# First strip of a two-layer graph kernel: rows gathered at once into idle tiles, low parts partly on GpSimd, setup in few wide operations

## The chip, the cores and the metric

The kernel runs on one core of a Trainium2 chip. The metric is the device time of one execution in microseconds, lower is better; the number compared is the median of several runs.

The engines are TensorE (PE, with its weight loads PEld), VectorE (DVE), ScalarE (ACT), GpSimd (POOL) and SyncE (SP, which here only issues transfers). Each works through its own instructions in order; semaphores tie them together.

## The reference, cut to what matters

Two graph attention layers over 10,000 nodes and 20,000 edges (10,000 drawn ones, sorted by destination, and one self loop per node), then a small feed-forward block:

```python
xn = layernorm(x)                                  # x: [10000, 768] f32
def gat(x, W, a_src, a_dst, b, heads, d_out, concat):
    h = (x @ W).reshape(N, heads, d_out)
    e = leaky_relu(einsum(h, a_src)[src] + einsum(h, a_dst)[dst], 0.2)
    alpha = softmax_over_edges_of_each_dst(e)      # segment max, exp, segment sum
    out = segment_sum(alpha[:, :, None] * h[src], dst)
    return (out.reshape(N, heads * d_out) if concat else out.mean(axis=1)) + b
h = elu(gat(xn, W1, ..., heads=4, d_out=512, concat=True))   # [10000, 2048]
x = x + gat(h, W2, ..., heads=1, d_out=768, concat=False)
out = x + ffn(layernorm(x))                        # 768 -> 96 -> 768, gelu
```

The kernel moves the weighted sum ahead of the first product: for each head it computes z = sum over edges of alpha * xn[src], and then z @ W1. Numbers are kept to near f32 precision by writing each f32 operand as a high and a low f16 part and adding three f16 products (high*high, high*low, low*high).

## The kernel before, in words

Stages follow each other with a barrier between: logits of layer 1, softmax over edges (it leaves one record of 16 numbers per edge in DRAM), `stage_layers` (both matrix products, by far the longest), a second softmax, and the output stage. The change is inside `stage_layers`, and there only in its beginning.

`stage_layers` works in 20 strips of 500 nodes (`NS`, `SN`). A strip has 10 windows of 50 nodes (`WPS`, `WN`). One window's tile has 128 partitions: 78 for edges that end in the window and 50 for its own nodes. For each window q, i:

- `load_slots` (L1142) brings the ten records tiles into `slots`, one transfer each, and the nodes' mean and 1/deviation by one transfer from `logit1` (L1148). In the first strip ACT issues half of the records (L1462).
- `slot_math` (L1242) makes the ten columns of row indices `idx`, and `mean`, `scale`, `bias`. Then come ten masks (L1273), ten look-up products on PE (L1480), the weights and their halves `wh`, `wl` (L1278 to L1282).
- `gather` on POOL (L1195) fetches 128 rows of x by index into `raw[:, i % 2]`, a tile with two buffers. A buffer is free again when the window two before has been multiplied (`z_done`).
- `high_rows` on ACT (L1433) writes the normalised rows as f16 into `rows_hi[:, i % 2]`; `low_rows` on DVE (L1267, L1268) normalises `raw` in place and subtracts the high part, in place again (`rows_lo` is the same memory as `raw`).
- `spread` on DVE (L1289 to L1293) makes the 128 x 200 weight tiles `ah`, `al`.
- `window` on PE (L1491) makes 18 products of 128x128 by 128x200 into the three banks `pz`; ACT takes each bank's high part to `zh` (L1425) and DVE its low part to `zl` (L1298).

In strips 1 to 19 the windows are made beside the products of the strip before. The ten windows of the first strip (L1399 to L1411, L1464 to L1468, L1562) have no such cover: nothing else runs, and the first product of `body(0)` (L1524) starts behind them. The order of DVE in that loop, by window i, is: rows of i+1, low parts of i, spread of i+2. ACT's is: high rows of i+1, high parts of i.

The tiles `gh` and `gl` (128 x 16 x 504 f16 each) are the input of the second layer's product. They are first written in `body(0)`, and stand idle while the first strip's windows are made. Their four last columns are only zeroed (L1219, L1221).

Ahead of all this DVE sets up constants (L1217 to L1239), 93 instructions, most of them one column wide; the semaphore `init` reaches 3 behind the last of them, and SP and ACT wait for it before they load records, since the records land in the tile `slots`, which these instructions write.

Of the kernel before, what the change touches and what calls it, by code (L numbers as in the profile page):

```python
# [24 lines left out]
ALU = mybir.AluOpType  # L25
ACT = mybir.ActivationFunctionType
# [995 lines left out]

STEPS = NT * KC
XPER = 25
AT_STEP = {1 + 6 * i: i for i in range(WPS)}
# [67 lines left out]
def stage_layers(nc, c, io, dr):  # L1093
    with ExitStack() as ctx:
# [12 lines left out]
        step_off, step_self = m.sb("step_off", [128, 1]), m.sb("step_self", [128, 1])  # L1107
        place, posi = m.sb("place", [128, 1]), m.sb("posi", [128, 128], I32)
        pos = m.sb("pos", [128, 128])
        idx = m.sb("idx", [128, WPS], I32)  # L1110
# [23 lines left out]
            "h2_out", "scale_ready", "hi_done", "normed", "lo_done", "xrows_ready"))  # L1134
        b2_in, x_copied = m.sem("b2_in"), m.sem("x_copied")
        block = ctx.enter_context(nc.Block())
# [5 lines left out]
        def _(sp):  # L1142
            def load_slots(q, first):
                if not first:
                    sp.wait_ge(a_ready, WPS * q)
                for i in range(WPS // 2 if first else WPS):
                    load_records(sp, c, LAYER1, dr.rec1, slots, slots_in, WPS * q + i, i)
                sp.dma_start(slots[WE:128, :, 11:13],  # L1148
                             dr.logit1[bass.ds(SN * q, SN), 2 * HEADS:TW1].rearrange("(i p) w -> p i w", p=WN),
                             allow_slow_non_contiguous=True).then_inc(slots_in, 16)  # L1150

# [20 lines left out]
            sp.dma_start(b2[:, 0:D], io["b2"].rearrange("(a d) -> a d", a=1).broadcast_to([128, D])).then_inc(b2_in, 16)  # L1172
            sp.wait_ge(init, 3)
            load_slots(0, True)
# [8 lines left out]
        @block.gpsimd  # L1183
        def _(pool):
            nc.gpsimd.iota(posi[:], pattern=[[1, 128]], base=-WE, channel_multiplier=0).then_inc(posed, 1)
            nc.gpsimd.iota(idx[:, 0:1], pattern=[[0, 1]], base=-WE, channel_multiplier=1).then_inc(posed, 1)

            def hold(sem, value):

                pool.wait_ge(sem, value)  # L1190
                pool.sem_inc(held, 1)

            pool.wait_ge(posed, 2)

            def gather(q, first):  # L1195
                hold(idx_ready, q + 1)
                for i in range(WPS):
                    if not (first and i < 2):
                        hold(z_done, 3 * (WPS * q + i - 1))
                    nc.gpsimd.indirect_dma_start(raw[:, i % 2, :], None, io["x"][:, :], bass.IndirectOffsetOnAxis(  # L1200
                        ap=idx[:, i:i + 1], axis=0), bounds_check=N - 1, oob_is_err=False).then_inc(gathered[i % 2], 16)

            def extra_chunk(i, w, k):
                hold(xidx_ready, 2 * k + 2)
                nc.gpsimd.indirect_dma_start(raw[:, 0, :], None, io["x"][:, :], bass.IndirectOffsetOnAxis(
                    ap=xidx[:, 0:1], axis=0), bounds_check=N - 1, oob_is_err=False).then_inc(xgathered, 16)

            gather(0, True)
            windows_with_extras(pool, c, LAYER1, 0, WPS, extra_chunk)
            with pool.Fori(1, NS) as q:  # L1210
                gather(q, False)
                windows_with_extras(pool, c, LAYER1, WPS * q, WPS, extra_chunk)

        @block.vector
        def _(dve):

            ch = Chain(dve, setup)  # L1217
            nc.vector.memset(raw[:], 0.0).then_inc(init, 1)
            nc.vector.memset(gh[:, :, SN:], 0.0).then_inc(init, 1)  # L1219
            nc.vector.memset(b2[:, D:W2C], 0.0)  # L1220
            nc.vector.memset(gl[:, :, SN:], 0.0)  # L1221
            dve.wait_ge(posed, 2)
            ch.put(nc.vector.tensor_copy(pos[:], posi[:]))
            ch.put(nc.vector.memset(slots[:], 0.0))
            ch.link(nc.vector.tensor_copy(place[:], idx[:, 0:1]))
            ch.put(nc.vector.tensor_scalar(is_self[:], place[:], 0.0, None, ALU.is_ge))
            ch.link(nc.vector.tensor_scalar(is_edge[:], place[:], 0.0, None, ALU.is_lt))
            ch.put(nc.vector.tensor_scalar(step_off[:], is_edge[:], float(-SN), None, ALU.mult))
            ch.put(nc.vector.tensor_scalar(step_self[:], is_self[:], float(SN), None, ALU.mult))
            nc.vector.memset(xslots[:], 0.0).then_inc(xslots_free, 1)  # L1230
# [8 lines left out]
            nc.vector.memset(near[:], 0.0).then_inc(init, 1)  # L1239
            per = 13 + WPS  # L1240

            def slot_math(qc, q, first):  # L1242

                dve.wait_ge(slots_in, 16 * (WPS + 1) * (q + 1))
                if not first:
                    for b in range(2):
                        dve.wait_ge(gathered[b], 16 * (WPS // 2) * q)
                qc.put(nc.vector.tensor_tensor(rel[:], slots[:, :, 9], woff[:], ALU.add))
# [102 lines left out]
            def body(s, first, last):  # L1351
                q = s + 1
                gc = Chain(dve, chain, KC * s)
                qc = Chain(dve, setup, q * per + ch.n)
                rc = Chain(dve, normed, WPS * q)
                for k in range(KC):
# [46 lines left out]
            spread(qc, 0, 1, True)  # L1403
            rc = Chain(dve, normed)
            low_rows(rc, 0, 0)
            for i in range(WPS):
                if i + 1 < WPS:
                    low_rows(rc, 0, i + 1)
# [12 lines left out]
        def _(act):  # L1421
# [6 lines left out]
            def high_rows(q, i):  # L1428

                if i < 2:  # L1430
                    act.wait_ge(scale_ready, q + 1)
                act.wait_ge(gathered[i % 2], 16 * (WPS // 2) * q + 16 * (i // 2 + 1))
                nc.scalar.activation(rows_hi[:, i % 2], raw[:, i % 2], ACT.Identity, bias=bias[:, i:i + 1],  # L1433
# [26 lines left out]

            act.wait_ge(init, 3)
            for i in range(WPS // 2, WPS):  # L1462
                load_records(act, c, LAYER1, dr.rec1, slots, slots_in, i, i)
            high_rows(0, 0)  # L1464
            for i in range(WPS):
                if i + 1 < WPS:
                    high_rows(0, i + 1)
                high_parts(0, i)  # L1468
# [6 lines left out]
        def _(pe):  # L1475
# [5 lines left out]

            def window_products(d, b):

                o = pz[d // 2][:, d % 2 * HEADS * WN:(d % 2 + 1) * HEADS * WN]
                high, low = (part[:, b, 128 * d:128 * d + 128] for part in (rows_hi, rows_lo))
                flat = lambda t: t[:, b].rearrange("p h n -> p (h n)")
# [4 lines left out]
            def window(q, i, first):  # L1491
# [4 lines left out]
                for k in range(3):  # L1496
                    if not (first and i == 0):
                        pe.wait_ge(zl_ready, 3 * (WPS * q + i - 1) + k + 1)
                    for d in (2 * k, 2 * k + 1):
                        ins = window_products(d, i % 2)  # L1500
                    ins.then_inc(z_done, 1)
# [60 lines left out]
            for i in range(WPS):  # L1562
                window(0, i, True)
            pe.wait_ge(zl_ready, 3 * WPS)
            z_extras(0, None)
            body(0, True, False)
# [569 lines left out]
```

## Time and profile before

| | |
|---|---|
| median of 3 runs | 4033.67 us (4027.44 to 4034.61) |
| the profiled execution | 4030.57 us, of which its span 4028.8 us |
| stage_layers: first instruction | 447.66 us |
| last setup instruction of DVE ends | 455.44 us |
| first gather issued on POOL | 466.35 us |
| first window product on PE | 475.79 us |
| last low part of the ten windows ends | 529.14 us |
| first product of the first strip's body | 530.99 us |

The times in the last six lines are read from the timeline, as microseconds from the span's start. The timeline has one line per group of instructions: start, duration, engine, line of the kernel, operation, output and inputs, shapes, count, and in brackets how long the engine sat idle before it and what released it. Over the whole span PE is busy 89%, DVE 61%, ACT 38% and POOL 18%.

### The profile page before, as it was taken

How to read it: one execution, taken by the hardware profiler on the slowest of the kernel's cores; microseconds unless marked ns; L12 is line 12 of the kernel's file. 1: busy time of each engine (PE TensorE's matmuls, PEld its weight loads, DVE VectorE, ACT ScalarE, POOL GpSimd, SP SyncE). 2: the span in 40 equal slices, each digit the busy share in tenths (PEclk: the TensorE clock that was granted, in tenths of full speed). 3: DMA queues.
4: the chain of work that ended last, by engine and by line, in shares of the span. 5: the costliest groups of instructions: out<-in, count | busy, mean ns of one | idle time of the engine just before them, and what ended most of it. 6: DMA issues, size and time to landing. Idle time of an engine off the chain costs nothing. (4 is left out here: it accounts for less than half of the span.)

```text
span 4028.8 us, 67552 instructions
## 1 busy us (share of the span) xinstructions
PE 3600.7 (89%) x21929; PEld 2143.5 (53%) x21930; DVE 2472.8 (61%) x5700; ACT 1524.8 (38%) x2491; POOL 724.3 (18%) x1254
## 2 busy tenths in 40 slices
PE   5844289999999999999999999999999996499898
PEld 3321146655655665565566556556556654266555
DVE  8977555554565465455546545555654634699998
ACT  2322143443344344334334434433443433244444
POOL 0047100000000010000000000000000000276665
PEclk9977589999999999999999999999999998699999
DMA  8630112111111211111111121111111100378887
GB/s 228 150 93 4 30 39 60 37 40 50 42 45 41 56 41 37 57 36 46 44 42 51 38 59 37 44 47 41 49 39 57 42 24 14 91 224 238 232 243 216
DMA packets 147070, 302.39 MB, mean 75 GB/s; under 512 B 84557, under 2 KB 84636, under 8 KB 142572
## 3 DMA queue, kind: packets, MB, share of 16 engines
q1 hardware_dynamic: 118041, 205.18, 17.5%
q0 software_dynamic: 27520, 92.78, 8.6%
q8 instruction: 198, 3.24, 0.4%
q14 instruction: 136, 1.11, 0.1%
q10 hardware_dynamic: 1175, 0.07, 0.0%
HBM read 260.49 MB, written 93.94 MB: 88 GB/s over the span
## 5 line engine op out<-in xcount | busy, mean ns | idle before, releaser
L1548 PE MATMUL lay_pm<-w,lay_gh 128*128 128x512 f16 x2560 | 903.4, 378 | 0.0
L1524 PE MATMUL lay_pm<-lay_zh,w1h 128*128 128x500 f16 x1920 | 718.8, 374 | 28.3 <-DVE lay_h L1390 22.9
L1526 PE MATMUL lay_pm<-lay_zh,w1l 128*128 128x500 f16 x1920 | 718.9, 374 | 0.0
L1525 PE MATMUL lay_pm<-lay_zl,w1h 128*128 128x500 f16 x1920 | 718.8, 374 | 0.0
L1549 PE MATMUL lay_pm<-w,lay_gh 128*128 128x258 f16 x2560 | 699.5, 273 | 0.0
L1200 POOL DMA_INDIRECT lay_raw<-in_x_dram,lay_idx x200 | 210.1, 1050 | 2556.7 <-PE lay_pz L1489 1626.3
L1442 ACT ACTIVATE lay_ex<-lay_pm,b1c,scale 128x500 f32<-128x500 f32 x320 | 245.5, 767 | 835.7 <-PE lay_pm L1526 835.7
L1548 PE MATMUL lay_pm<-w,lay_gl 128*128 128x512 f16 x1280 | 483.9, 378 | 0.0
L1433 ACT ACTIVATE lay_rows_hi<-lay_raw,lay_bias,lay_scale 128x768 f16<-128x768 f32 x200 | 205.0, 1025 | 691.7 <-DMA lay_raw<-in_x_dram,lay_idx 691.7
L1342 DVE TENSOR_SCALAR lay_ex<-lay_ex,scale 128x500 f32<-128x500 f32 x320 | 153.7, 480 | 495.4 <-ACT lay_ex L1442 493.1
L1548 PEld LDWEIGHTS lay_pm<-w,lay_gh 128*128 128x128 f16 x2560 | 250.7, 98 | 281.4
L1298 DVE SCALAR_TENSOR_TENSOR lay_zl<-lay_pz,lay_zh 128x400 f16<-128x400 f32 x600 | 307.7, 566 | 117.9 <-ACT lay_zh L1425 117.9
L1425 ACT ACTIVATE lay_zh<-lay_pz 128x400 f16<-128x400 f32 x600 | 296.0, 503 | 219.2 <-PE lay_pz L1489 215.2
L1267 DVE TENSOR_SCALAR lay_raw<-lay_raw,lay_mean,lay_scale 128x768 f32<-128x768 f32 x200 | 135.5, 678 | 375.5 <-ACT lay_rows_hi L1433 374.9
L1549 PE MATMUL lay_pm<-w,lay_gl 128*128 128x258 f16 x1280 | 349.9, 273 | 0.0
L1487 PE MATMUL lay_pz<-lay_ah,lay_rows_hi 128*128 128x200 f16 x1200 | 305.0, 254 | 26.8 <-DVE lay_zl L1298 22.4
L1524 PEld LDWEIGHTS lay_pm<-lay_zh,w1h 128*128 128x128 f16 x1920 | 195.6, 102 | 239.8 <-DVE lay_h L1388 31.5
L1488 PE MATMUL lay_pz<-lay_al,lay_rows_hi 128*128 128x200 f16 x1200 | 305.4, 254 | 0.0
L1489 PE MATMUL lay_pz<-lay_ah,lay_raw 128*128 128x200 f16 x1200 | 305.2, 254 | 0.0
L1526 PEld LDWEIGHTS lay_pm<-lay_zh,w1l 128*128 128x128 f16 x1920 | 187.7, 98 | 218.1 <-issue 1.3
L1525 PEld LDWEIGHTS lay_pm<-lay_zl,w1h 128*128 128x128 f16 x1920 | 187.7, 98 | 204.8 <-issue 1.1
L1344 DVE SCALAR_TENSOR_TENSOR lay_y<-lay_ex,scale,lay_y 128x500 f32<-128x500 f32 x320 | 236.4, 739 | 79.4 <-ACT lay_y L1444 79.4
(328 smaller groups left out, 5546.7 us busy)
## 6 DMA issues: line engine op xcount, KB each, us to landing
x<-in_x_dram SPq DMA_DIRECT2D x20, 1500.0 KB, 6.7
out_x<-x SPq DMA_DIRECT2D x100, 288.0 KB
out_own<-h SPq DMA_DIRECT2D x100, 288.0 KB
out_dram<-out_x SPq DMA_DIRECT2D x100, 288.0 KB
lgt_x<-in_x_dram SPq DMA_DIRECT2D x20, 1344.0 KB
h<-lay_h SPq DMA_DIRECT2D x80, 336.0 KB
w<-in_L_gnn_W_dram SPq DMA_DIRECT2D x6, 1024.0 KB, 13.5
sm_wraw<-in_L_gnn_W_dram SPq DMA_DIRECT2D x16, 384.0 KB, 9.2
```

Source lines behind the costliest of these rows:

```text
L1298: nc.vector.scalar_tensor_tensor(out=window_shape(zl, k, i), in0=pz[k][:, 0:2 * HEADS * WN].rearrange("p (k n) -> p k n", n=WN), scalar=1. ...
L1344: nc.vector.scalar_tensor_tensor(out=y[:, k % 2], in0=ex[:, k % 2], scalar=c.scale[:, 10:11], in1=y[:, k % 2], op0=ALU.add, op1=ALU.max).t ...
L1425: nc.scalar.activation(window_shape(zh, k, i), pz[k][:, 0:2 * HEADS * WN].rearrange("p (k n) -> p k n", n=WN), ACT.Copy, scale=1.0 / SA).t ...
L1442: nc.scalar.activation(ex[:, k % 2], p, ACT.Exp, bias=c.b1[:, k:k + 1], scale=c.scale[:, 8:9])\
L1487: pe.matmul(o, high, flat(ah), start=True, stop=False)
L1488: pe.matmul(o, high, flat(al), start=False, stop=False)
L1489: return pe.matmul(o, low, flat(ah), start=False, stop=True)
L1524: pe.matmul(o, c.w1h[:, d, cols], zh[:, d, h], start=(d == 0), stop=False)
L1525: pe.matmul(o, c.w1h[:, d, cols], zl[:, d, h], start=False, stop=False)
L1526: ins = pe.matmul(o, c.w1l[:, d, cols], zh[:, d, h], start=False, stop=(d == DC - 1))
L1548: pe.matmul(oa[:], x[:, k, nodes], wt[:, k, 0:512], **go)
L1549: ins = pe.matmul(ob[:, 0:D + 2 - 512], x[:, k, nodes], wt[:, k, 512:D + 2], **go)
```

## The change

- The ten gathers of the first strip no longer go to the two buffers of `raw` but each to a place of its own, `ahead[i]`: five in `gh`, five in `gl`, all issued in a row as soon as the indices are there. Each has a semaphore of its own (`came`).
- Since indices beyond the window are skipped by the gather, the places must hold zeros first: POOL zeroes both tiles whole at the stage's start.
- The first strip's normalising and low parts work in place in `ahead[i]`. Windows 0 to 2 keep both steps on DVE. For windows 3 to 9 the subtraction goes to POOL (`ON_POOL = 3`), behind the ten gathers in its queue.
- The one-column operations of DVE's setup become wide ones (over `steps`, an iota on POOL), and those that the record loads wait for stand first; `init` is waited for at 2.
- The mean and deviation of the first strip's nodes are loaded by POOL instead of SP.
- The zeroing of the last columns of `gh` and `gl` moves behind the first strip's windows; PE waits for it (`tails`).

```diff
+ON_POOL = 3
...
+        halves = [t[:].rearrange("p k n -> p (k n)") for t in (gh, gl)]
+        ahead = [halves[i // (WPS // 2)][:, 2 * D * (i % (WPS // 2)):2 * D * (i % (WPS // 2) + 1)] for i in range(WPS)]
...
         @block.gpsimd
+            nc.gpsimd.iota(stepi[:], pattern=[[WN, WPS]], base=0, channel_multiplier=0).then_inc(posed, 1)
+            for half in halves:
+                nc.gpsimd.memset(half.bitcast(F32), 0.0).then_inc(posed, 1)
...
+            pool.wait_ge(posed, 5)
+            def gather_ahead():
+                pool.wait_ge(init, 2)
+                nc.gpsimd.dma_start(slots[WE:128, :, 11:13],
+                                    dr.logit1[0:SN, 2 * HEADS:TW1].rearrange("(i p) w -> p i w", p=WN),
+                                    allow_slow_non_contiguous=True).then_inc(stats_in, 16)
+                hold(idx_ready, 1)
+                for i in range(WPS):
+                    nc.gpsimd.indirect_dma_start(ahead[i].bitcast(F32), None, io["x"][:, :], bass.IndirectOffsetOnAxis(
+                        ap=idx[:, i:i + 1], axis=0), bounds_check=N - 1, oob_is_err=False).then_inc(came[i], 16)
...
-            gather(0, True)
+            gather_ahead()
+            for i in range(ON_POOL, WPS):
+                pool.wait_ge(hi_done, i + 1)
+                pool.wait_ge(normed_ahead, i + 1)
+                nc.gpsimd.tensor_tensor(ahead[i][:, 0:D], ahead[i].bitcast(F32), rows_hi[:, i % 2], ALU.subtract)\
+                    .then_inc(lo_done, 1)
...
         @block.vector
-            for i in range(WPS):
-                ch.put(nc.vector.memset(xoff[:, i:i + 1], float(SN - WN * i)))
-                ch.put(nc.vector.tensor_scalar(woff[:, i:i + 1], is_edge[:], float(-WN * i), None, ALU.mult))
-                ch.put(nc.vector.tensor_scalar(wself[:, i:i + 1], place[:], float(WN * i), is_self[:, 0:1], ALU.add, ALU.mult))
-                for h in range(HEADS):
-                    ch.put(nc.vector.tensor_copy(slots[:, i, h:h + 1], is_self[:]))
-                ch.put(nc.vector.tensor_scalar(slots[:, i, 9:10], place[:], 0.0, None, ALU.max))
...
+            def low_rows_ahead(i):
+                at = ahead[i].bitcast(F32)
+                dve.wait_ge(hi_done, i + 1)
+                nc.vector.tensor_scalar(at, at, mean[:, i:i + 1], scale[:, i:i + 1], ALU.subtract, ALU.mult)\
+                    .then_inc(normed_ahead, 1)
+                if i < ON_POOL:
+                    dve.wait_ge(normed_ahead, i + 1)
+                    nc.vector.tensor_tensor(ahead[i][:, 0:D], at, rows_hi[:, i % 2], ALU.subtract).then_inc(lo_done, 1)
...
+            nc.vector.memset(gh[:, :, SN:], 0.0).then_inc(tails, 1)
+            nc.vector.memset(gl[:, :, SN:], 0.0).then_inc(tails, 1)
...
         @block.scalar
+            def high_rows_ahead(i):
+                act.wait_ge(came[i], 16)
+                if i >= 2:
+                    act.wait_ge(z_done, 3 * (i - 1))
```

GpSimd at the start of the stage, the kernel before: two iotas, then the ten gathers of the first strip (`lay_raw`), then the test for windows with more edges than fit.

```order
L1183 UNCONDITIONAL_BRANCH
L1185 IOTA lay_posi 128x128
L1186 IOTA lay_idx 128x1
L1200 DMA lay_raw<-in_x_dram,lay_idx 128x768 x10
L1044 TENSOR_LOAD table
```

The same engine and place, the changed kernel:

```order
L1192 IOTA lay_posi 128x128
L1193 IOTA lay_idx 128x1
L1194 IOTA lay_stepi 128x10
L1196 MEMSET lay_gh 128x4032
L1196 MEMSET lay_gl 128x4032
L1207 DMA lay_slots<-logit 50x10x2
L1212 DMA lay_gh<-in_x_dram,lay_idx 128x768 x5
L1212 DMA lay_gl<-in_x_dram,lay_idx 128x768 x5
L1231 TENSOR_TENSOR lay_gh<-lay_gh,lay_rows_hi 128x768 x2
L1231 TENSOR_TENSOR lay_gl<-lay_gl,lay_rows_hi 128x768 x5
```

Two large memsets and a small load now stand ahead of the gathers, and seven subtractions behind them.

VectorE's setup in the changed kernel, up to the last instruction that the record loads wait for (before, 93 instructions stood here, from L1218 to L1239; `lay_slots` is written first and the counters `lay_woff`, `lay_wself`, `lay_xoff` after):

```order
L1242 MEMSET lay_slots 128x160
L1244 CAST lay_place<-lay_idx 128x1
L1245 CAST lay_steps<-lay_stepi 128x10
L1246 TENSOR_SCALAR lay_is_self<-lay_place 128x1
L1247 TENSOR_SCALAR lay_is_edge<-lay_place 128x1
L1248 COPY lay_slots<-lay_is_self 128x10x4
L1250 TENSOR_SCALAR lay_slots<-lay_place 128x10
L1251 MEMSET lay_near 128x50
```

The 1536-column memset of `lay_raw` has moved from the first place to behind these, and 40 one-column copies have become one.

## Rows read from the trace of the kernel before

**Rows 1.** The page: busy time, share of the span, instructions of one engine.
```profile
PE 3600.7 (89%) x21929; PEld 2143.5 (53%) x21930; DVE 2472.8 (61%) x5700; ACT 1524.8 (38%) x2491; POOL 724.3 (18%) x1254
```
**Rows 2.** Waits in 447 to 531 us: engine, waited for, total, times, longest.
```profile
ACT lay_rows_hi L1433 <- DMA lay_raw<-in_x_dram,lay_idx: 61.9, 10, 39.3
```
**Rows 3.** Timeline, setup of the stage, up to the first gather.
```profile
447.85 0.13 POOL L1186 IOTA lay_idx<- 128x1 int32 x1
448.02 1.34 DVE L1218 MEMSET lay_raw<- 128x1536 f32 x1 [4.54 <-PEq L112]
...
455.34 0.10 DVE L1239 MEMSET lay_near<- 128x50 uint32 x1
456.38 6.54 ACTq L1070 DMA_DIRECT2D lay_slots<-rec  x5
...
464.46 0.17 DVE L1248 TENSOR_TENSOR lay_rel<-lay_slots,lay_woff 128x10 f32<-128x10 f32 x1 [9.03 <-DMA lay_slots<-logit]
...
466.35 1.02 POOL L1200 DMA_INDIRECT lay_raw<-in_x_dram,lay_idx  x1 [18.37 <-DVE lay_idx L1254]
```
**Rows 4.** Timeline, start of the output stage: a large GpSimd memset and VectorE beside it.
```profile
3474.16 6.49 POOL L1823 MEMSET out_rows<- 128x7680 f32 x1
...
3476.43 4.30 DVE L1866 CAST out_pos<-out_posi 128x100 f32<-128x100 int32 x1
```
**Rows 5.** Small gathers on POOL (L906): ns min/median/max, and time to landing.
```profile
L906 POOL DMA_INDIRECT sm_gdst<-logit,dsts x79: 992/997/3400, 306.9 to 416.9; - x79
...
DMA to landing us min/median/max: 2.3/2.4/4.8
```
**Rows 6.** Groups of VectorE by shape, 400 to 560 us: busy us, mean ns.
```profile
L1298 DVE SCALAR_TENSOR_TENSOR lay_zl<-lay_pz,lay_zh 128x400 f16<-128x400 f32 x30 | 15.7, 567 | 2.9 <-ACT lay_zh L1425 2.9
L1268 DVE TENSOR_TENSOR lay_raw<-lay_raw,lay_rows_hi 128x768 f16<-128x768 f32 x10 | 9.6, 958 | 0.3
L1267 DVE TENSOR_SCALAR lay_raw<-lay_raw,lay_mean,lay_scale 128x768 f32<-128x768 f32 x10 | 6.8, 677 | 13.9 <-ACT lay_rows_hi L1433 13.9
```
**Rows 7.** Timeline, the first strip's windows: rows landing, first products of windows.
```profile
470.37 1.03 ACT L1433 ACTIVATE lay_rows_hi<-lay_raw,lay_bias,lay_scale 128x768 f16<-128x768 f32 x1 [39.31 <-DMA lay_raw<-in_x_dram,lay_idx]
...
472.39 1.03 ACT L1433 ACTIVATE lay_rows_hi<-lay_raw,lay_bias,lay_scale 128x768 f16<-128x768 f32 x1 [0.99 <-DMA lay_raw<-in_x_dram,lay_idx]
...
475.79 0.33 PE L1487 MATMUL lay_pz<-lay_ah,lay_rows_hi 128*128 128x200 f16 x1 [4.40 <-DVE lay_raw L1268]
...
479.83 1.00 POOL L1200 DMA_INDIRECT lay_raw<-in_x_dram,lay_idx  x1 [11.15 <-PE lay_pz L1489]
...
483.80 1.03 ACT L1433 ACTIVATE lay_rows_hi<-lay_raw,lay_bias,lay_scale 128x768 f16<-128x768 f32 x1 [4.31 <-DMA lay_raw<-in_x_dram,lay_idx]
...
487.16 0.33 PE L1487 MATMUL lay_pz<-lay_ah,lay_rows_hi 128*128 128x200 f16 x1 [5.25 <-DVE lay_zl L1298]
...
489.94 0.37 PE L1489 MATMUL lay_pz<-lay_ah,lay_raw 128*128 128x200 f16 x1
...
520.97 0.32 PE L1487 MATMUL lay_pz<-lay_ah,lay_rows_hi 128*128 128x200 f16 x1 [5.63 <-DVE lay_zl L1298]
```
**Rows 8.** Timeline, a window at the upper clock: its first and last product.
```profile
513.63 0.25 PE L1487 MATMUL lay_pz<-lay_ah,lay_rows_hi 128*128 128x200 f16 x1 [0.90 <-DVE lay_zl L1298]
...
515.09 0.25 PE L1489 MATMUL lay_pz<-lay_ah,lay_raw 128*128 128x200 f16 x1
```
**Rows 9.** PE by stretches: us, PE busy (x), granted clock, DMA share, GB/s.
```profile
481.00:484.00 3.00, 0.91 (x6) 0.88 0.34 102
```
**Rows 10.** Timeline, a gather on POOL and the VectorE instruction beside its end.
```profile
491.20 1.00 POOL L1200 DMA_INDIRECT lay_raw<-in_x_dram,lay_idx  x1 [7.40 <-PE lay_pz L1489]
491.75 0.43 DVE L1289 TENSOR_SCALAR lay_near<-lay_pos,lay_rel 128x50 f16<-128x50 f32 x1
```
**Rows 11.** Timeline, the end of the windows and the first product of the body.
```profile
528.57 0.57 DVE L1298 SCALAR_TENSOR_TENSOR lay_zl<-lay_pz,lay_zh 128x400 f16<-128x400 f32 x1 [0.42 <-ACT lay_zh L1425]
530.99 0.60 PE L1524 MATMUL lay_pm<-lay_zh,w1h 128*128 128x500 f16 x1 [3.00 <-issue]
```

More of the change, by code:

```diff
@@ L1108, in stage_layers @@
         place, posi = m.sb("place", [128, 1]), m.sb("posi", [128, 128], I32)
+        stepi, steps = m.sb("stepi", [128, WPS], I32), m.sb("steps", [128, WPS])
         pos = m.sb("pos", [128, 128])
@@ L1134, in stage_layers @@
             "h2_out", "scale_ready", "hi_done", "normed", "lo_done", "xrows_ready"))
-        b2_in, x_copied = m.sem("b2_in"), m.sem("x_copied")
+        b2_in, x_copied, tails, normed_ahead, stats_in = (m.sem(n) for n in (
+            "b2_in", "x_copied", "tails", "normed_ahead", "stats_in"))
+        came = [m.sem(f"came{i}") for i in range(WPS)]
         block = ctx.enter_context(nc.Block())
@@ L1191, in hold, with gather @@
                 pool.sem_inc(held, 1)
-            pool.wait_ge(posed, 2)
-            def gather(q, first):
+            pool.wait_ge(posed, 5)
[8 more added lines that the diff above has]
+                        ap=idx[:, i:i + 1], axis=0), bounds_check=N - 1, oob_is_err=False).then_inc(came[i], 16)
+            def gather(q):
                 hold(idx_ready, q + 1)
                 for i in range(WPS):
-                    if not (first and i < 2):
-                        hold(z_done, 3 * (WPS * q + i - 1))
+                    hold(z_done, 3 * (WPS * q + i - 1))
                     nc.gpsimd.indirect_dma_start(raw[:, i % 2, :], None, io["x"][:, :], bass.IndirectOffsetOnAxis(
@@ L1217, in _ @@
             ch = Chain(dve, setup)
[L1218 to L1223, printed above, removed]
             ch.put(nc.vector.memset(slots[:], 0.0))
-            ch.link(nc.vector.tensor_copy(place[:], idx[:, 0:1]))
+            dve.wait_ge(posed, 3)
@@ L1226, in _ @@
+            ch.put(nc.vector.tensor_copy(place[:], idx[:, 0:1]))
+            ch.link(nc.vector.tensor_copy(steps[:], stepi[:]))
             ch.put(nc.vector.tensor_scalar(is_self[:], place[:], 0.0, None, ALU.is_ge))
             ch.link(nc.vector.tensor_scalar(is_edge[:], place[:], 0.0, None, ALU.is_lt))
+            ch.put(nc.vector.tensor_copy(slots[:, :, 0:HEADS], is_self[:].rearrange("p (a b) -> p a b", a=1)
+                                         .broadcast_to([128, WPS, HEADS])))
+            nc.vector.tensor_scalar(slots[:, :, 9], place[:].broadcast_to([128, WPS]), 0.0, None, ALU.max).then_inc(init, 1)
@@ L1228, in _ @@
+            nc.vector.memset(near[:], 0.0).then_inc(init, 1)
             ch.put(nc.vector.tensor_scalar(step_off[:], is_edge[:], float(-SN), None, ALU.mult))
             ch.put(nc.vector.tensor_scalar(step_self[:], is_self[:], float(SN), None, ALU.mult))
+            ch.put(nc.vector.tensor_scalar(xoff[:], steps[:], -1.0, float(SN), ALU.mult, ALU.add))
+            ch.put(nc.vector.tensor_scalar(woff[:], steps[:], -1.0, is_edge[:, 0:1], ALU.mult, ALU.mult))
+            ch.put(nc.vector.tensor_scalar(wself[:], steps[:], place[:, 0:1], is_self[:, 0:1], ALU.add, ALU.mult))
@@ L1238, in _ @@
+            nc.vector.memset(b2[:, D:W2C], 0.0)
             ch.wait()
-            nc.vector.memset(near[:], 0.0).then_inc(init, 1)
             per = 13 + WPS
             def slot_math(qc, q, first):
[L1244 to L1247, printed above, removed]
+                if first:
+                    dve.wait_ge(slots_in, 16 * WPS)
+                    dve.wait_ge(stats_in, 16)
+                else:
+                    dve.wait_ge(slots_in, 16 * (WPS + 1) * q + 16 * WPS)
+                    if not isinstance(q, int) or q > 1:
+                        for b in range(2):
+                            dve.wait_ge(gathered[b], 16 * (WPS // 2) * (q - 1))
@@ L1480, in look_up, with window_products @@
                 pe.matmul(look[:, i], mask[:, i % 2], slots[:, i, 4:9], start=True, stop=True).then_inc(looked, 1)
-            def window_products(d, b):
+            def window_products(d, b, low_part=None):
                 o = pz[d // 2][:, d % 2 * HEADS * WN:(d % 2 + 1) * HEADS * WN]
-                high, low = (part[:, b, 128 * d:128 * d + 128] for part in (rows_hi, rows_lo))
+                high, low = (part[:, 128 * d:128 * d + 128] for part in (
+                    rows_hi[:, b], rows_lo[:, b] if low_part is None else low_part))
                 flat = lambda t: t[:, b].rearrange("p h n -> p (h n)")
@@ L1499, in window @@
                     for d in (2 * k, 2 * k + 1):
-                        ins = window_products(d, i % 2)
+                        ins = window_products(d, i % 2, ahead[i] if first else None)
                     ins.then_inc(z_done, 1)
```

33 lines of the change are left out of this document (20 added, 13 removed).

## The prediction

> **What bounds the kernel now.** I read the page first: PE is busy 89% of the span [rows 1], so almost everything after the first body product is bound by PE, and a change in the first strip's windows can only be worth what lies between the start of this stage and that product. I then read the timeline of that stretch, 447.66 to 530.99 us. It has two parts. Up to 475.79 the windows' first product waits for a chain: DVE's setup (to 455.44), five record loads each on ACT and SP (ACT's queue ends at 456.38 + 6.54 = 462.92), `lay_rel` at 464.46, the first gather at 466.35, its rows on ACT at 470.37 [rows 3, 7]. From 475.79 to 529.14 run ten windows [rows 7, 11], 53.35 us. The waits say who ends last there: ACT waits for gathered rows 61.9 us in ten pieces, 22.6 of them apart from the first [rows 2]. PE works in pairs of windows, since `raw` has two buffers: the windows 2 and 8 start at 487.16 and 520.97 [rows 7], so a pair takes 33.81 / 3 = 11.27 us. In it, a gather issued 0.9 us behind the last product takes 3.97 us to its rows (479.83 to 483.80) [rows 7]; that is the wait that the change takes out.
>
> **Part 1, gathers ahead.** With ten places, all gathers go out from 466.35 on, 1.33 us apart, the last at 478.3. The first two rows landed 2.02 us apart (470.37 and 472.39) though issued 1.33 apart [rows 7], so I take 2.02 us for each further one: the tenth is there at 488.5, long before its window. Bound from the other side: 3.97 us each, the latency of one alone, and the tenth is there at 506.1; also just in time, as the sum below shows. So the gather leaves the chain. What is late next is a loop over two windows: the last product of window i, then ACT's high part, DVE's low part, `spread`, DVE's normalising of window i+2, the subtraction, and window i+2's products. `rows_hi` has two buffers still, so ACT's high rows of i+2 also wait for window i, but ACT ends them (0.38 + 1.03) ahead of DVE's `spread`.
>
> **Part 2, the loop's length.** A window of 18 products takes 487.16 to 489.94 + 0.37 = 3.15 us at the lower clock of 1.2 GHz and 513.63 to 515.09 + 0.25 = 1.71 us at the upper one of 2.4 GHz [rows 7, 8]. ACT's high part costs 0.53 up to DVE's start, DVE's low part 0.48 (of 0.57, the rest overlaps what follows), `spread` 0.91, normalising 0.71 [rows 6]. The subtraction on POOL, L, shows in no row. From below, one pass over 768 columns at the rate of POOL's memset (6.49 us / 7680 = 0.845 ns a column [rows 4]) is 0.65 us; from above, three passes, two inputs and one output, are 1.95 us, and with some 0.2 us of fixed cost 2.15. I take two passes and the fixed cost, 1.5 us, because both inputs must be read and the write can run beside it; plus 0.1 for the semaphore. DVE does the same in 0.96 [rows 6]. The loop is 3.15 + 0.53 + 0.48 + 0.91 + 0.71 + 1.6 = 7.4 us per pair at the lower clock, against 11.27. POOL is free of its gathers at 479.3, and its first subtraction is due at 485.6, so the queue order costs nothing; it would from 6.3 us of delay on.
>
> By the Trainium skill, GPSIMD Engine Reference, section Elementwise, a `tensor_tensor` of 2048 f32 columns takes 4497 ns on GpSimd; scaled to 768 that is an estimate of 1.7 us. No row of this trace shows it. By it the sum would be 0.8 us longer.
>
> **Part 3, the windows' sum.** Windows 0 and 1 run as before, to 481.9. Window 2's rows are then waiting: normalising and subtraction on DVE end at 482.5. Window 3: DVE does low parts of 1 (1.5), spread (0.9), normalising (0.7), POOL subtracts: 487.2. From there three loops for windows 5, 7, 9: 487.2 + 3 x 7.4 = 509.4, plus 3.15 for window 9 and 1.15 for its last bank's high and low part: 513.7 at the lower clock throughout. At the upper clock the loop is 6.0 and the end 487.2 + 18.0 + 1.7 + 1.15 = 508.0. The granted clock rose to 0.88 of the stretch 481 to 484, after six microseconds of products with no gap [rows 9]. Now products come denser, so I take half of the way, 511.0. Beside the gathers' last part some of DVE's instructions are held up: `lay_near` took 0.43 us instead of 0.24 and ended with the gather, 492.18 against 492.20 [rows 10]. Nine gathers now fall on masks, weights and first rows: up to 9 x 0.2; I take 1.0. End at 512.0 instead of 529.14: **17.1 us less**. The two memsets of the tail columns (0.1 us together in the setup now) come behind the last low part: 0.1 more.
>
> **Part 4, the setup, where I expect nothing.** The wide operations are about eight instructions ahead of `init` instead of 93: if they ran freely, `init` would come at 449.3 instead of 455.44. But POOL begins its memset of `gh` right behind its iotas, near 448.0 [rows 3]. Two memsets of 4032 columns at 0.845 ns are 3.4 us each, to 454.9. In the output stage a memset of POOL ran from 3474.16 to 3480.65, and DVE's small cast beside it, 100 columns that should take some 0.2 us, lasted 4.30 us and ended at 3480.73, just behind the memset [rows 4]. The cast of `stepi` (L1245) is of the same kind and starts after the memset has begun; the copy into `slots` (L1248) is one too. If DVE gets in between the two memsets, the cast is held to 451.5 and the copy to 454.9, and `init` comes at 455.4; if not, the cast is held to 454.9 and `init` comes at 456.1. Both ends beside 455.44 before: 0 to 0.7 us later; I take 0.3. The same rows exclude a gain only while the casts are held; without that see the first rival.
>
> The Trainium skill, SBUF, section "Who interferes with whom", has that rule: VectorE in a two-port mode and GpSimd exclude each other for a whole instruction, whoever is first. By that rule the setup gains nothing, and the trace agrees with its 4.30 us.
>
> The load of mean and deviation leaves SP (one issue of 0.3 us), but ACT's five record loads end at 462.92 as before, so `lay_rel` still starts 9.0 us behind `init` [rows 3]. On POOL that load has 500 small pieces; a gather of 128 takes 1.0 us and lands after 2.4 [rows 5], so at worst 3.9 + 2.4 behind `init`, that is 6.3 of 9.0 us: hidden by the records, with 2.7 us to spare.
>
> **Sum.** 17.1 - 0.1 - 0.3 = 16.7 us less. The profiled execution's span goes from 4028.8 to 4012.1 and its time from 4030.57 to 4013.9. The median of the runs shown lies 3.1 us above that execution: **4017 us**. Everything behind the first body product moves up as a block; SP's ten record loads of strip 1 start with the windows' last `spread`, so they move up too.
>
> **Rivals.**
> 1. *The setup pays too.* DVE isn't held by POOL's memsets (small or broadcast operands might use one port only). Then `init` comes at 449.3 and records are in at 458.3; but POOL's load starts only at 454.9 and lands by 458.3 to 461.2. Gain 3.3 to 6.1 us more: 4012. Against it speaks the 4.30 us cast [rows 4]. Chance 0.14.
> 2. *POOL's subtraction is slow or held up* by DVE's work on the same memory. From 487.2 on each microsecond of L costs one per loop and one in window 3, 4.0 us in all. L = 4 gives 4027. For it: POOL has no row with two wide inputs. Chance 0.12.
> 3. *Slower than before*: the same place, decided at L = 1.5 + 16.7 / 4.0 = 5.7 us, where POOL's subtraction is longer than the gather it replaces in the loop. At L = 8 the time is 4043. Against it: ten times one pass at the memset's rate. Chance 0.03.
> 4. *The gathers aren't ahead in effect*: rows land 3.97 us apart, the tenth at 506.1; then its high part, normalising, subtraction, products and parts (1.03 + 0.71 + 1.6 + 3.15 + 1.15) end at 513.7, 1.7 us later than I take: 4019, inside my own range.
>
> **How the numbers follow.** My forecast, 4009 to 4023 with rival 4 in it, has 0.71; its ends are the upper clock throughout, L of 0.65 and no hold-ups (3.0 + 3.4 + 1.0 us better) and the lower clock, L of 2.15 and full hold-ups (2.7 + 2.6 + 0.8 us worse). Rival 1 has 0.14, rival 2 0.12, rival 3 0.03. The range 4005 to 4027 takes in the forecast, rival 1 and half of rival 2. About 0.2%, 8 us, is what a measurement of this kernel can tell from no change: faster by more than that are the forecast, rival 1 and the smaller part of rival 2 (L below 3.7), 0.88; within it 0.09; slower 0.03.
>
> **What would show it.** In the changed kernel's timeline: the cast of `stepi` lasting 3 us or more, or the copy into `slots` doing so; `init`'s last instruction ending between 455.4 and 456.2; `lay_rel` 9 us behind it; ten gathers in a row with no wait for products; POOL's subtraction near 1.5 us; window starts 3.7 us apart or less, and the first product of the body near 514. The setup's part is wrong if the cast takes 0.2 us. The windows' part is wrong if POOL's subtraction is above 3 us, or if ACT still waits for gathered rows behind window 2.

## The result and the profile after

The changed kernel is **slower by 0.3%**: 4041.47 us median of 7 runs (4036.56 to 4049.55) beside 4032.17 us (4026.33 to 4034.61), ratio 1.0029 with a 95% interval of 1.0016 to 1.0042. 4017 us was forecast, 16.7 less than the 4033.67 known then. The profiled execution took 4045.95 us, its span 4044.1, that is 15.3 us more than before.

The beginning went as forecast. The timeline of the changed kernel's setup on GpSimd and VectorE (start, duration, engine, line, operation; in brackets the idle time before and what ended it), which answers to [rows 3]:

```profile
448.30 3.45 POOL L1196 MEMSET lay_gh<- 128x4032 f32 x1
...
448.46 3.32 DVE L1245 CAST lay_steps<-lay_stepi 128x10 f32<-128x10 int32 x1
...
451.70 3.48 POOL L1196 MEMSET lay_gl<- 128x4032 f32 x1
...
452.06 3.15 DVE L1248 COPY lay_slots<-lay_is_self 128x40 f32<-128x40 f32 x1
...
455.13 0.10 DVE L1251 MEMSET lay_near<- 128x50 uint32 x1
...
463.89 0.17 DVE L1274 TENSOR_TENSOR lay_rel<-lay_slots,lay_woff 128x10 f32<-128x10 f32 x1 [6.78 <-DMA lay_slots<-rec]
...
465.87 1.08 POOL L1212 DMA_INDIRECT lay_gh<-in_x_dram,lay_idx  x1 [8.95 <-DVE lay_idx L1280]
```

Ten columns cast in 3.32 us, forty copied in 3.15: both are held, and end 0.03 us behind the end of a memset of GpSimd (451.75 and 455.18). `init` is there at 455.23 (455.44 before). TensorE's windows and the first product of the body, which answer to [rows 7, 8, 11]:

```profile
482.74 0.25 PE L1535 MATMUL lay_pz<-lay_ah,lay_rows_hi 128*128 128x200 f16 x1 [1.94 <-DVE lay_zl L1334]
486.88 0.33 PE L1535 MATMUL lay_pz<-lay_ah,lay_rows_hi 128*128 128x200 f16 x1 [1.46 <-ACT lay_rows_hi L1508]
...
503.79 0.25 PE L1535 MATMUL lay_pz<-lay_ah,lay_rows_hi 128*128 128x200 f16 x1 [1.39 <-POOL lay_gl L1231]
506.88 0.25 PE L1535 MATMUL lay_pz<-lay_ah,lay_rows_hi 128*128 128x200 f16 x1 [1.39 <-POOL lay_gl L1231]
511.78 0.60 PE L1572 MATMUL lay_pm<-lay_zh,w1h 128*128 128x500 f16 x1 [3.20 <-issue]
```

No window behind the first two waits for a gather, from 494.49 on they start 3.1 us apart, and the body begins at 511.78 instead of 530.99: **19.2 us earlier**. The last product of the first layer in the 20 strips, however, comes at 3309.94 instead of 3296.96. Between these two, 32.2 us were lost, in a stretch whose work the diff doesn't touch; the 2.3 us that are missing to 15.3 lie behind it. The loss is in every pass: the strips' loop has 17 heads with an idle time in view, and from one to the next lie 142.4 us on average before (142.9 at most) and 144.4 after (143.4 at least). The head of one pass, the first product that it makes, first before, then after:

```profile
959.09 0.37 PE L1524 MATMUL lay_pm<-lay_zh,w1h 128*128 128x500 f16 x1 [1.36 <-DVE lay_h L1390]
```

```profile
942.68 0.37 PE L1572 MATMUL lay_pm<-lay_zh,w1h 128*128 128x500 f16 x1 [2.82 <-issue]
1086.30 0.37 PE L1572 MATMUL lay_pm<-lay_zh,w1h 128*128 128x500 f16 x1 [2.69 <-issue]
1808.63 0.58 PE L1572 MATMUL lay_pm<-lay_zh,w1h 128*128 128x500 f16 x1 [3.01 <-issue]
```

Before, the profile names VectorE as the one that TensorE waited for. Now the wait is longer, and the profile names nobody ("issue"); VectorE's `lay_h` was done 0.07 us ahead of the head before and 1.54 us ahead of it after:

```profile
958.54 0.48 DVE L1390 SCALAR_TENSOR_TENSOR lay_h<-lay_pm,scale,lay_b 128x258 f32<-128x258 f32 x1
```

```profile
940.66 0.48 DVE L1426 SCALAR_TENSOR_TENSOR lay_h<-lay_pm,scale,lay_b 128x258 f32<-128x258 f32 x1
```

And behind six of the 17 heads the clock falls as well, before behind none. Granted clock (the number ahead of the last two) behind the head at 1808.63 and behind that of the same pass before:

```profile
1808.63:1813.63 5.00, 5.00 (x13) 1.80 (x14) 0.00 (x0) 0.00 (x0) 0.00 (x0) 0.50 0.18 45
```

```profile
1813.60:1818.60 5.00, 5.00 (x24) 2.35 (x25) 0.13 (x1) 0.93 (x2) 0.00 (x0) 1.00 0.34 84
```

13 products in 5 us at half the clock (1.2 GHz), 24 at 2.4 GHz. The page gives the sum over all heads (busy us, mean ns, idle before us), and section 3 a second trace of the same thing (packets, MB, share). Before:

```profile
q8 instruction: 198, 3.24, 0.4%
L1524 PE MATMUL lay_pm<-lay_zh,w1h 128*128 128x500 f16 x1920 | 718.8, 374 | 28.3 <-DVE lay_h L1390 22.9
```

After:

```profile
q8 instruction: 215, 3.52, 0.4%
L1572 PE MATMUL lay_pm<-lay_zh,w1h 128*128 128x500 f16 x1920 | 723.6, 377 | 49.6 <-issue 49.6
```

21.3 us more idle time. The other 10.9 I put down to stretches at the lower clock, as the one above: the six passes that begin with one take 144.9 to 146.4 us, the others 143.4 to 144.0, which makes 10.3 us. The queue that carries instructions brought 17 packets more, one for each of the loop's 17 jumps back. A packet has 16,384 bytes (3.24 MB / 198). That it holds 256 instructions is an assumption here, which the runs with 256 instructions more test.

**Theory A**: the change puts one instruction more, `pe.wait_ge(tails, 2)`, ahead of TensorE's loop over strips. That shifts the whole loop by one place in the instruction stream, and the shifted loop has a costlier jump back. **Rival B**: the change itself disturbs the later strips (another order of GpSimd's or VectorE's work, the wait on the tails). **Rival C**, written down for the later runs: every instruction added ahead of the loop makes it slow.

### The profile page after: what moved, and what is told of

It is laid out like the page before. It is cut to its first block and busy times, and to the rows that moved or that the text cites. A ratio compares the mean times of both kernels' runs of the same rounds, so it can differ in the third digit from the quotient of the medians.

```text
span 4044.1 us, 67670 instructions
## 1 busy us (share of the span) xinstructions
PE 3606.4 (89%) x21929; PEld 2144.7 (53%) x21930; DVE 2468.0 (61%) x5619; ACT 1526.1 (38%) x2491; POOL 752.9 (19%) x1265
## 5 line engine op out<-in xcount | busy, mean ns | idle before, releaser
L1470 ACT ACTIVATE lay_rows_hi<-lay_raw,lay_bias,lay_scale 128x768 f16<-128x768 f32 x190 | 194.8, 1025 | 624.8 <-DMA lay_raw<-in_x_dram,lay_idx 624.8
L1537 PE MATMUL lay_pz<-lay_ah,lay_raw 128*128 128x200 f16 x1140 | 283.9, 249 | 0.0
```

Source lines behind the costliest of these rows:

```text
L1537: return pe.matmul(o, low, flat(ah), start=False, stop=True)
```

## Experiments

Ratios are to the kernel before, run on the same chip in the same session; intervals are 95%. On the chips of the first four and of the last four runs the stages ahead of the change take some 40 us longer in every trace (the kernel before, of which none was taken there, ran 4070.37 and 4071.29 us); only ratios, and times within a run, are compared.

**The change without its added instruction.** VectorE zeroes the tail columns ahead of its last low part, for which TensorE waits anyway; the extra wait goes.

```diff
+                    if tails_too and k == 2:
+                        nc.vector.memset(gh[:, :, SN:], 0.0)
+                        nc.vector.memset(gl[:, :, SN:], 0.0)
...
-            nc.vector.memset(gh[:, :, SN:], 0.0).then_inc(tails, 1)
-            nc.vector.memset(gl[:, :, SN:], 0.0).then_inc(tails, 1)
...
-            pe.wait_ge(tails, 2)
```

> The changed kernel, but TensorE's one added instruction ahead of its loop over strips (the wait for the zeroed tail columns) is gone: VectorE zeroes them ahead of the last low part of the first strip, which TensorE waits for anyway. TensorE's instructions then stand at the same places as in the kernel before. Theory A (the place of TensorE's loop in its code costs some 1.8 us per pass, 18 passes): the loss in the strips goes, the first strip's 19 us stay, 4013 us; strips last 142.4 us again and TensorE's gap at the head of a pass is near 1.45 us. Rival B (something else that the change does, on GpSimd, VectorE or in the queues, disturbs later strips): 4041 us as the changed kernel, gaps of 2.7 us.

Measured: 4053.45 us beside 4070.37, ratio 0.9954 (0.9942 to 0.9967). Its page and the head of a pass:

```profile
q8 instruction: 198, 3.24, 0.4%
L1573 PE MATMUL lay_pm<-lay_zh,w1h 128*128 128x500 f16 x1920 | 718.9, 374 | 27.3 <-DVE lay_h L1429 19.4
```

```profile
977.77 0.37 PE L1573 MATMUL lay_pm<-lay_zh,w1h 128*128 128x500 f16 x1 [1.59 <-DVE lay_h L1429]
```

Packets, idle time and duration are those of before, and 4033.67 x 0.9954 would be 4015 us, 2 from the forecast (the interval is 4010 to 4020). The change is worth what was forecast; one instruction takes it away.

**The kernel before with one instruction more.**

```diff
             pe.wait_ge(zl_ready, 3 * WPS)
+            for _ in range(1):
+                pe.wait_ge(init, 2)
```

> The kernel before with one thing added: TensorE waits once more, ahead of the loop over strips, for a semaphore that has long been reached. It costs nothing in itself. Theory A (place of the code): every pass of the loop gets 1.2 to 1.9 us longer, 4060 to 4065 us, and the page counts about 17 more packets in the instruction queue (198 before, 215 after). Rival B: within 0.1% of before, 4032 us.

Measured: 4099.66 us, ratio 1.0071 (1.0059 to 1.0084). A wait that has long been fulfilled, run once, costs 29 us:

```profile
q8 instruction: 215, 3.52, 0.4%
L1524 PE MATMUL lay_pm<-lay_zh,w1h 128*128 128x500 f16 x1920 | 721.3, 376 | 48.2 <-issue 48.2
```

Rival B falls: nothing of the change is in this kernel, and it has the whole loss.

**GpSimd's memsets behind `init`.** The first kernel of this section, with the two memsets moved behind the wait for `init` and the load of mean and deviation.

```diff
-            for half in halves:
-                nc.gpsimd.memset(half.bitcast(F32), 0.0).then_inc(posed, 1)
...
                                     allow_slow_non_contiguous=True).then_inc(stats_in, 16)
+                for half in halves:
+                    nc.gpsimd.memset(half.bitcast(F32), 0.0).then_inc(posed, 1)
+                pool.wait_ge(posed, 5)
```

> As the run without the tail wait, and GpSimd's two memsets of the idle tiles come behind the semaphore that releases the record loads, and behind its own small load, instead of at the stage's start. They then run while the records travel (9 us), and VectorE's setup ahead of the record loads is not held. Lock theory: that setup ends near 449.3 instead of 455.2, the index math starts near 459 instead of 463.9, and the time is 4 to 6 us below the run without the tail wait, 4007 to 4009 us. Rival: the memsets now hold VectorE's rest of the setup until 457 and delay something else as much: no gain, 4013 us.

Measured: 4042.37 us, ratio **0.9933** (0.9920 to 0.9946), the fastest kernel of this study; the kernel before and the changed one are both beaten. Its setup:

```profile
488.07 0.23 POOL L1192 IOTA lay_posi<- 128x128 int32 x1 [67.94 <-POOLq L112]
...
488.58 0.16 DVE L1246 CAST lay_steps<-lay_stepi 128x10 f32<-128x10 int32 x1
...
489.24 0.10 DVE L1252 MEMSET lay_near<- 128x50 uint32 x1
...
499.96 1.08 POOL L1213 DMA_INDIRECT lay_gh<-in_x_dram,lay_idx  x1 [2.09 <-DVE lay_idx L1281]
...
546.33 0.60 PE L1574 MATMUL lay_pm<-lay_zh,w1h 128*128 128x500 f16 x1 [3.04 <-issue]
```

The same cast takes 0.16 us instead of 3.32. From GpSimd's first iota to `init` are 1.3 us instead of 7.3, to the first gather 11.9 instead of 17.9, to the first product of the body 58.3 instead of 62.3 in the kernel with the memsets first. So the wide setup is worth 4.0 us once no memset stands on it. The gathers go out 6.0 us earlier; two of these are lost again in the windows, whose first and last start lie 32.4 us apart here and 30.1 in the kernel with the memsets first. The medians differ by 11 us; 7 of the profiled spans' 11.7 us lie behind the strips (730.9 against 737.9 us), where the kernels are equal, and where the profiled runs of this study scatter from 728 to 739. Only the 4 are claimed.

**All subtractions on VectorE.** As the first kernel, with

```diff
-ON_POOL = 3
+ON_POOL = 10
```

> As the run without the tail wait, with all ten subtractions of the first strip on VectorE, none on GpSimd. GpSimd's subtraction took 1.64 us in the changed kernel against 0.96 on VectorE. If the loop over two windows sets the pace (my prediction's part 2), the subtraction on VectorE makes that loop 0.8 us shorter but takes VectorE's time between the other steps: within 2 us of the run without the tail wait, 4012 to 4015 us. If GpSimd's part carries the gain, it is 4 us or more slower than that run.

Measured: 4052.20 us, ratio 0.9956 (0.9943 to 0.9969): not told apart from the first kernel, so the medians decide between neither of the two expectations. In the trace windows are 3.87 us apart instead of 3.10, and the body begins 68.9 us behind the first iota instead of 62.3. Of these 6.6 us one comes back at once, since TensorE's clock is still up when the body begins (0.39 us a product and a granted clock of 0.72 over the first 6 us, against 0.60 and 0.50). What becomes of the other five is within what these medians can tell. GpSimd's part is then worth 5 us by the trace, and 0 give or take 7 by the medians.

**Where the loop may lie.** Eight kernels move it further, without other effect. Four have n waits ahead of the wait for `zl_ready`, the other four right behind TensorE's first wait on `init`, where it then idles for 10 us. The kernel before took 4033.31 us beside the first four and 4071.29 us beside the last four.

```diff
+            for _ in range(n):
+                pe.wait_ge(init, 2)
             pe.wait_ge(zl_ready, 3 * WPS)
```

The kernel before with 16, 50 and 100 of them, and the changed one with 99:

> The kernel before with 16 redundant waits (on init, long fulfilled) in TensorE's stream between the first strip's windows and the wait for zl ahead of its loop over strips, where TensorE idles. Theory A (placement in the 16.4 KB blocks in which the instructions come): the loop is about 1,858 instructions of 64 bytes long (990 counted in the program, and 862 products that are issued as weight load and product, and a few more), that is 7 blocks and some 66 instructions, so it touches 8 blocks or 9. The kernel before touches 8, ending just short of a border; with 1 instruction more it touched 9 (17 packets more). With 16 it must still touch 9: 215 packets, gap ahead of the first product of each pass 2.4 to 3.1 us, ratio 1.006 to 1.008. Rival D (only a loop whose last instruction stands alone in a fresh block is slow): 215 packets, but gaps back at 1.2 to 1.9 us and ratio 1.000. Rival C (each added instruction costs for itself): ratio above 1.007, growing with the number.

> As before, with 50 such waits. Theory A: 50 is still less than the some 66 instructions by which the loop's start has to move to the next border, so 9 blocks: 215 packets, gaps 2.4 to 3.1 us, ratio 1.006 to 1.008. Since the 66 is a count with a few instructions of doubt, 198 packets and ratio 1.000 would say that the overhang is under 50. Rival D: 215 packets, ratio 1.000. Rival C: ratio above that of 16 waits.

> As before, with 100 such waits. Theory A: the loop's start has passed the border too, so it touches 8 blocks again: 198 packets, gaps 1.2 to 1.9 us that end on DVE's lay_h, ratio 0.999 to 1.001, although there are 99 instructions more than in the slow kernel. Rival C: ratio above 1.007, the slowest of the three. Rival D: ratio 1.000 as well (told apart by 16 and 50).

> The changed kernel, its wait on the tails kept, with 99 redundant waits more at the same place, so its loop lies where that of the kernel before with 100 lies. Theory A: 198 packets, gaps 1.2 to 1.9 us ending on DVE's lay_h, and the change shows what it is worth: ratio 0.9945 to 0.9965, as without the wait. If the wait on the tails itself, or the order of GpSimd's and VectorE's work, made the passes longer (rival B), it stays at 1.002 to 1.004.

The last four: the kernel before with 256, 150 and 200, the changed one with 255:

> The kernel before with 256 redundant waits on init right behind TensorE's first one, where it then waits 10 us for the masks. 256 instructions of 64 bytes are one whole block of 16.4 KB, so the loop over strips lies as in the kernel before. Theory A: 199 packets (one more, once), gaps of 1.2 to 1.9 us ahead of each pass that end on DVE's lay_h, ratio 0.999 to 1.001, although 256 instructions are added. Rival C (each instruction more ahead of the loop makes it slow, wherever it then lies, or the kernel before is fast by a lucky coincidence of another kind): 215 packets or more, ratio 1.006 to 1.010, as with 1, 16, 50 and 100.

> As before with 150 waits at that place. With 100 the loop touched 9 blocks, where my count of the loop's length (an overhang of 66) had let me expect 8, so the overhang is over 100. Theory A: either 198 packets and ratio 0.999 to 1.001 (overhang 101 to 150) or 215 and 1.007 to 1.010 (overhang above); whichever it is, packets and time must go together. Rival C: 215 and slow.

> As before with 200 waits. Theory A: 198 packets and ratio 0.999 to 1.001 if the overhang is under 200, else 215 and 1.007 to 1.010; never fast at 150 and slow at 200. Rival C: 215 and slow.

> The changed kernel, its wait on the tails kept, with 255 redundant waits more at that place: with the one that the change adds they are 256, one whole block, so its loop lies as in the kernel before. Theory A: 199 packets, gaps of 1.2 to 1.9 us ending on DVE's lay_h, ratio 0.9945 to 0.9965, as without the wait: 32 us less than the changed kernel loses in its passes, by adding instructions. Rival C or B: 215 or more packets and a ratio of 1.002 to 1.005.

Measured, ordered by the shift of the loop against the kernel before (packets per pass counted between two heads):

| shift | kernel | ratio (95%) | packets in all | per pass |
|---|---|---|---|---|
| 0 | before | 1 | 198 | 9 |
| 0 | changed, no wait on tails | 0.9954 (0.9942 to 0.9967) | 198 | 9 |
| 1 | before + 1 | 1.0071 (1.0059 to 1.0084) | 215 | 10 |
| 1 | changed | 1.0029 (1.0016 to 1.0042) | 215 | 10 |
| 16 | before + 16 | 1.0091 (1.0071 to 1.0111) | 215 | 10 |
| 50 | before + 50 | 1.0090 (1.0073 to 1.0107) | 215 | 10 |
| 100 | before + 100 | 1.0096 (1.0076 to 1.0116) | 215 | 10 |
| 100 | changed + 99 | 1.0037 (1.0023 to 1.0052) | 215 | 10 |
| 150 | before + 150 | 1.0066 (1.0049 to 1.0083) | 215 | 10 |
| 200 | before + 200 | 0.9995 (0.9985 to 1.0005) | 100 | 2, in three passes 9 |
| 256 | before + 256 | 0.9993 (0.9983 to 1.0002) | 79 | 2 |
| 256 | changed + 255 | 0.9955 (0.9938 to 0.9971) | 79 | 2 |

256 instructions more cost nothing, one costs 0.7%: rival C falls. It isn't the other place of the last four either, since 150 at that place are slow. Rival D of the expectations (only a loop whose last instruction stands alone in a fresh block is slow) falls with 16, which are as slow as one. The changed kernel with its wait on the tails kept and 255 further waits is at 0.9955 where the changed kernel is at 1.0029, and equal to the one without the wait. Theory A's main point, that the time goes by the loop's place within 256 instructions, holds in every kernel of the table.

Two parts of it don't. My count of the loop's overhang, 66 instructions, was wrong: both kernels with a shift of 100 were expected fast and are slow, 150 is slow too, 200 is fast, so the border lies between 151 and 200. And packets and time don't go together as I had it: I expected 199 packets for the shift of 256 and there were 79. The page of the changed kernel with 255 waits:

```profile
q8 instruction: 79, 1.29, 0.1%
L1573 PE MATMUL lay_pm<-lay_zh,w1h 128*128 128x500 f16 x1920 | 719.0, 374 | 24.0 <-DVE lay_h L1426 11.1
```

Seven packets fewer in each pass than before, and 0.2 us won (142.24 us a pass in the kernel before with 256 waits, against 142.43): those packets come beside the work and cost next to nothing. What costs is a stall at one place. The kernel with 150 waits shows that it is tied to a place in the stream and not to the loop's head:

```profile
996.83 0.37 PE L1525 MATMUL lay_pm<-lay_zh,w1h 128*128 128x500 f16 x1 [1.21 <-DVE lay_h L1388]
...
998.09 0.37 PE L1525 MATMUL lay_pm<-lay_zh,w1h 128*128 128x500 f16 x1
999.68 0.37 PE L1526 MATMUL lay_pm<-lay_zl,w1h 128*128 128x500 f16 x1 [1.22 <-issue]
```

Here the head comes as early as in a fast kernel, and TensorE then stands still for 1.22 us after seven products, some twenty instructions behind the head. If that is the border between two blocks, it lies 150 + 20 behind the loop's old start, which agrees with slow at 150 and fast at 200.

**The jump itself** is in the trace. It is an instruction of its own, COMPARE_BRANCH, in the sequencer that feeds TensorE (`PEldq`). Its durations in ns (shortest/median/longest; the shortest is the one at the loop's end that isn't taken) in the kernel before, the changed one, the kernel before + 1 and the changed one + 255:

```profile
L1567 PEldq COMPARE_BRANCH  x18: 83/3604/3904, 812.8 to 3234.1; - x18
```

```profile
L1616 PEldq COMPARE_BRANCH  x18: 83/4754/5143, 793.8 to 3247.2; - x18
```

```profile
L1569 PEldq COMPARE_BRANCH  x18: 83/4668/5207, 851.2 to 3298.8; - x18
```

```profile
L1617 PEldq COMPARE_BRANCH  x18: 82/3490/3692, 835.8 to 3252.5; - x18
```

In the six kernels with shifts of 1 to 100 the median jump takes 4.67 to 4.92 us, in all others 3.46 to 3.60. In all kernels the first product of the pass starts 0.37 to 0.45 us behind the jump's end. So it is the jump for which TensorE waits at the head, and VectorE, which the profile names in the kernel before, only gets done at nearly the same time.

The instruction queue's packets that start during one such jump, first in the kernel before (955.29 to 958.72 us), then in the changed one (937.37 to 942.31 us):

```profile
q8 instruction: 1, 0.02, 1.9%
```

```profile
q8 instruction: 2, 0.03, 5.0%
```

So it is in all 17 jumps: two packets in the six kernels with shifts of 1 to 100, one in all others, the one with 150 waits among them. By the shares (of 16 engines' time in the stretch) one packet's transfers add up to 1.0 us and the two to 4.0, so each of the two is slower than one alone. In the kernel with 150 waits a packet starts between the jump's end and the end of the stall (996.46 to 999.68 us):

```profile
q8 instruction: 1, 0.02, 2.2%
```

This packet takes from 997.23 to 998.36, and TensorE goes on 1.3 us behind its end. In the kernel before the packet takes from 956.30 to 957.33, and the jump ends 1.4 us behind that.

**What stays open**: why a second packet is fetched during the jump in some places of the loop, and which instructions it holds. That the jump waits for its packets is read from times that fit in every pass; no record says it outright.

## Why the prediction was wrong

The step that failed is in its sum: "Everything behind the first body product moves up as a block". It moved up by 19.2 us and lost 32.2 on the way. The added wait on the tails was costed as 0.1 us of memsets; as an instruction of TensorE ahead of a loop of 18 passes it had no price, and no rival either. In its place the runs showed a jump back of 4.75 us instead of 3.60 in each of 17 passes (21.3 us more idle time) and, behind six of them, stretches at the lower clock (some 10 us). The one rival on the slower side was another mechanism (GpSimd's subtraction longer than 5.7 us, 0.03) and is refuted by the 1.64 us measured.

By its steps:

- **Part 1**, gathers ahead: right. Most go out 1.30 us apart, ScalarE waits for rows of windows 0 and 1 only (high rows at 469.89 and 471.93).
- **Part 2**, the subtraction: forecast 1.5 + 0.1 us, measured 1.64 on GpSimd. By the Trainium skill, GPSIMD Engine Reference, section Elementwise, scaled to 768 columns, the estimate was 1.7; the trace agrees with its 1.64.

```profile
485.14 1.64 POOL L1231 TENSOR_TENSOR lay_gh<-lay_gh,lay_rows_hi 128x768 f16<-128x768 f32 x1 [5.79 <-DVE lay_gh L1300]
...
495.85 1.64 POOL L1231 TENSOR_TENSOR lay_gl<-lay_gl,lay_rows_hi 128x768 f16<-128x768 f32 x1 [1.46 <-DVE lay_gl L1300]
```

- **Part 3**, the windows: window 2 was forecast for 482.5 and 3 for 487.2, they came at 482.74 and 486.88. From window 3 to window 9 it took 20.0 us; half way between the clocks, as I took it, is 20.1 (22.2 and 18.0). The last low part ended at 509.73 instead of 512.0, 2.3 us to the good: the last window ran at 2.4 GHz (0.25 us a product; 0.7 us), window 3 started 0.3 us early, and the 1.0 us allowed for operations held up by the gathers didn't show in the end. Mis-sized were these terms, not the length of the loop.
- **Part 4**, the setup: right in its mechanism. `init` came at 455.23, 0.2 us ahead of the forecast 455.4 to 456.1. A cast and a copy were held by GpSimd's memsets, and the kernel with the memsets moved shows it by 0.16 us for the same cast against 3.32. By the Trainium skill, SBUF, section "Who interferes with whom", such operations and GpSimd's can exclude each other for a whole instruction; the trace agrees with these two numbers. Rival 1 (the setup pays too) is refuted for the change as it is, and its 3.3 to 6.1 us are about what came, 4.0, once the memsets moved. Not everything is held: operations of one column that started 0.1 us behind the start of a memset (448.30 and 451.70) took 0.15 us.

```profile
448.39 0.15 DVE L1244 CAST lay_place<-lay_idx 128x1 f32<-128x1 int32 x1 [0.16 <-POOL lay_stepi L1194]
...
451.82 0.15 DVE L1246 TENSOR_SCALAR lay_is_self<-lay_place 128x1 f32<-128x1 f32 x1
```

- The tails: `MEMSET` of both in 0.13 us behind the last low part, as forecast.

Without the shift of the loop the ratio was 0.9954 and 0.9955 in two kernels made in two ways, against 4017 / 4033.67 = 0.9959 forecast. That it agrees to 2 us is in part luck: the intervals are 5 to 7 us wide to each side, and in the trace the body began 19.2 us earlier where the sum had 16.7.

## What to carry to other kernels

When a change adds or removes instructions ahead of a hot loop, count them on each engine: a single redundant wait, run once, cost 1 us and more in every pass here, 29 us in all. A loss in each pass of a loop that nobody touched, with "issue" as its releaser at the loop's head, another count of instruction packets on the page and a longer jump back, can be this and not the change; take the instruction out elsewhere, or pad, before the change is judged. And a large memset on an idle GpSimd isn't free: put it where VectorE has nothing small to do that others wait for.

## What the runs showed of the hardware that was not expected

- TensorE's time per pass depends on where its loop lies within 256 instructions: shifts of 1, 16, 50, 100 and 150 were slow by 0.66 to 0.96%, shifts of 0, 200 and 256 were equal within 0.1%.
- The jump back at the end of a loop pass took TensorE's sequencer 3.46 to 3.60 us (medians) with one instruction packet fetched during it and 4.67 to 4.92 with two. TensorE's idle time at the head was 0.9 to 1.9 us in the first case and 2.4 to 3.1 in the second.
- The instruction traffic itself is hardly a price: passes with 9 and with 2 packets took 142.4 and 142.2 us.
- An idle time of 3.01 us at the head of a pass was followed by 13 products at half the clock, where one of 1.71 us was not. The length alone doesn't decide: one of 3.10 us (head at 1375.67) was followed by none. By the sum above up to a third of what the shift costs (10.9 of 32.2 us) goes with such stretches.
